# A mixture-of-experts layer with x and the weights laid out by the host, loaded by two queues, and the first products in another order

## The reference

```python
def _L0_cond_ref(hidden_states, gating_probs, shared_gate_prob, Wg, Wu, Wd, Sg, Su, Sd):
    E, B, S, D, F = (8, 2, 128, 128, 512)     # B is 16 here: x is (16, 128, 128)
    h = hidden_states
    g = jnp.einsum('bsd,edf->ebsf', h, Wg)
    u = jnp.einsum('bsd,edf->ebsf', h, Wu)
    expert_outs = jnp.einsum('ebsf,efd->ebsd', jax.nn.silu(g) * u, Wd)
    expert_output = jnp.einsum('be,ebsd->bsd', gating_probs, expert_outs)
    shared = jnp.einsum('bsf,fd->bsd', jax.nn.silu(h @ Sg) * (h @ Su), Sd)
    sg = shared_gate_prob[:, :, None]
    return (1.0 - sg) * expert_output + sg * shared

def _L1_cond_ref(x, fwd_steps, T):
    Tb = T[fwd_steps - 1]
    return jnp.einsum('bij,bjk->bik', Tb, x)

x = x + _L0_cond_ref(x, ...)
x = x + _L1_cond_ref(x, itok_B_1_98, L1_cond_T)
```

## Time and profile before

| what | value |
|---|---|
| median of 3 runs | 311.98 us (311.73 to 312.07) |
| the profiled execution, its own time | 312.09 us |
| its span in the trace | 310.1 us |
| PE busy | 305.5 us, 99% of the span |
| DVE, ACT, POOL busy | 217.5, 164.6, 102.2 us |
| moved by the DMA engines | 10.39 MB |

### The profile page before, as it was taken

One profiled execution on the slowest core, in us unless ns is written; L12 is line 12 of the kernel. 1 busy time (PEld: TensorE's weight loads), 2 busy tenths in 40 slices (PEclk: granted clock), 3 DMA queues, 4 the chain that ended last, 5 costly groups with the idle time before them and its releaser, 6 DMA issues.

```text
span 310.1 us, 4762 instructions
## 1 busy us (share of the span) xinstructions
PE 305.5 (99%) x1364; PEld 253.3 (82%) x1364; DVE 217.5 (70%) x355; ACT 164.6 (53%) x306; POOL 102.2 (33%) x116
## 2 busy tenths in 40 slices
PE   8999999999999999999999999999999999999996
PEld 7688888888888888888888888888888888888885
DVE  2786667766676666776667766677666766668885
ACT  5565555555555555555555555555555555555552
POOL 2565312441155115511552134411441155111310
PEclk9999999999999999999999999999999999999999
DMA  6930300030001100030003001100013000000112
GB/s 159 201 89 2 103 1 2 0 94 7 1 0 45 56 0 0 0 101 0 0 0 109 13 13 17 17 14 13 15 17 110 0 0 0 0 2 0 34 36 68
DMA packets 32727, 10.39 MB, mean 34 GB/s; under 512 B 16208, under 2 KB 32720, under 8 KB 32720
## 3 DMA queue, kind: packets, MB, share of 16 engines
q1 hardware_dynamic: 32720, 10.30, 13.5%
HBM read 9.25 MB, written 1.05 MB: 33 GB/s over the span
## 4 chain that ended last, share of the span: by engine, by line
PE 95%; SPq 1%; DMA 1%; POOL 0%; DVE 0%; ACT 0%; issue 0%
PE o_bank L470 11%; PE o_bank L473 11%; PE o_bank L471 11%; PE g_bank L446 10%; PE u_bank L446 10%; PE g_bank L445 10%; PE u_bank L445 10%; PE g_bank L444 10%; PE u_bank L444 10%; DMA w_raw<-in_L_cond_Wd 1%; PE o_bank L491 1%; SPq L158 1%; PE o_bank L483 0%; POOL w_lo L212 0%; DVE res L371 0%; PE u_bank L483 0%
## 5 line engine op out<-in xcount | busy, mean ns | idle before, releaser
L342 DVE TENSOR_TENSOR u_bank<-u_bank,silu_g 128x512 f32<-128x512 f32 x144 | 100.7, 699 | 84.2 <-PE u_bank L446 82.6
L278 ACT ACTIVATE silu_g<-g_bank 128x512 f32<-128x512 f32 x144 | 86.1, 598 | 132.8 <-PE g_bank L446 132.4
L348 DVE TENSOR_TENSOR h_lo<-u_bank,h_hi 128x512 fp32r<-128x512 f32 x144 | 97.9, 680 | 0.1
L260 POOL TENSOR_TENSOR acc<-acc,scaled 128x512 f32<-128x512 f32 x32 | 41.5, 1296 | 163.2 <-DVE scaled L356 163.0
L284 ACT ACTIVATE h_hi<-u_bank 128x512 fp32r<-128x512 f32 x144 | 85.4, 593 | 0.7 <-DVE u_bank L342 0.7
L470 PE MATMUL o_bank<-h_hi,w_hi 128*128 128x512 f32 x144 | 56.2, 390 | 0.8 <-POOL w_lo L212 0.8
L444 PE MATMUL u_bank<-x_hi,w_hi 128*128 128x512 f32 x144 | 56.1, 390 | 0.0
L473 PE MATMUL o_bank<-h_lo,w_hi 128*128 128x512 f32 x144 | 56.0, 389 | 0.0
L445 PE MATMUL u_bank<-x_lo,w_hi 128*128 128x512 f32 x144 | 56.0, 389 | 0.0
L471 PE MATMUL o_bank<-h_hi,w_lo 128*128 128x512 f32 x144 | 56.0, 389 | 0.0
L446 PE MATMUL u_bank<-x_hi,w_lo 128*128 128x512 f32 x144 | 56.0, 389 | 0.0
(11 more groups left out here) (49 smaller groups left out, 151.2 us busy)
## 6 DMA issues: line engine op xcount, KB each, us to landing
w_raw<-in_L_cond_Wd SPq DMA_DIRECT2D x8, 256.0 KB, 3.9
w_raw<-in_L_cond_Wg SPq DMA_DIRECT2D x7, 256.0 KB, 3.1
w_raw<-in_L_cond_Wu SPq DMA_DIRECT2D x7, 256.0 KB, 3.8
T_blk<-in_L_cond_T SPq DMA_DIRECT2D x64, 16.0 KB, 1.6
out_y<-res SPq DMA_DIRECT2D x3, 256.0 KB, 2.3
x_blk<-in_x SPq DMA_DIRECT2D x4, 128.0 KB, 3.6
x_nat<-in_x SPq DMA_DIRECT2D x1, 256.0 KB, 2.8
x_blk<-in_x SPq DMA_DIRECT2D x4, 64.0 KB, 2.7
```

The costliest lines, as they stand in the source:

```text
L260: nc.gpsimd.tensor_tensor(acc[:, t, :], acc[:, t, :], scaled[:, t % 2, :], ALU.add).then_inc(acc_done, 1)
L278: nc.scalar.activation(silu_g[:, k % 2, :], g_bank[k % 2][:, :], ACT.Silu).then_inc(g_read, 1)
L342: nc.vector.tensor_tensor(u_bank[k % HR][:, :], u_bank[k % HR][:, :], silu_g[:, k % 2, :], ALU.mult).then_inc(h_done, 1)
L348: nc.vector.tensor_tensor(h_lo[:, k % HR, :], u_bank[k % HR][:, :], h_hi[:, k % HR, :].bitcast(F32), ALU.subtract).then_inc(split_done, 1)
```

## The change

The host now hands over other layouts. `xT` is x with the features in front, so a tile is 128 rows of 2 KB and lands in `acc` itself. `W_all` holds for each expert, row and chunk the gate, up and down columns side by side, so an expert is one transfer. `TT` is T with each matrix turned, and it lands in `T_plus`, where POOL adds the identity in place. `side` holds gates and shares, repeated for all rows. The output is stored as rows, batches, features and turned on the host. The transposes of x and T on PE and DVE, and their buffers, are gone.

```diff
-            sp.dma_start(x_nat[:, :, :], x[0:BT, :, :].rearrange("b s d -> s b d")).then_inc(x_in[0], 16)
-            sp.dma_start(w_raw[:, 0, 0, 0, :], Wg[0, :, 0:P]).then_inc(wg0_in, 16)
-            sp.dma_start(w_raw[:, 0, 0, 1, :], Wu[0, :, 0:P]).then_inc(wu0_in, 16)
...
-            load_blocks(x_blk[:, BT:2 * BT, :], x[BT:2 * BT, :, :], [x_in[1]] * 4)
-            sp.dma_start(w_raw[:, 0, :, 2, :], Wd[0, :, :].rearrange("(c p) d -> p c d", p=P)).then_inc(wd0_in, 16)
...
+            load_x(0, 1, x_in[0])
+            sp.dma_start(w_raw[:, 0, 2:NC, 0:2, :], W_all[0, :, 2:NC, 0:2, :]).then_inc(wc0_in[2], 16)
+            sp.dma_start(w_raw[:, 0, :, 2, :], W_all[0, :, :, 2, :]).then_inc(wd0_in, 16)
+            load_x(1, 2, x_in[1])
+            sp.dma_start(side_b[:, :], side).then_inc(c_in, 16)
+            load_x(2, NT, x_in[2])
+            load_expert(1, slice(1, 2))
...
+            for c in range(2):
+                act.dma_start(w_raw[:, 0, c, 0:2, :], W_all[0, :, c, 0:2, :]).then_inc(wc0_in[c], 16)
             act.wait_ge(zero_done, 1)
             nc.scalar.activation(silu_0[:, :], zero[:, 0:1], ACT.Silu)
...
+            for c in range(2):
+                act.wait_ge(wc0_in[c], 16)
+                round_w0(c, slice(0, 2))
...
+            dve.wait_ge(x_in[0], 16)
+            nc.vector.tensor_copy(x_hi[:, 0, :], acc[:, 0, :]).then_inc(x_rounded, 1)
             dve.wait_ge(x_rounded, 1)
+            nc.vector.tensor_tensor(x_lo[:, 0, :], acc[:, 0, :], x_hi[:, 0, :].bitcast(F32), ALU.subtract).then_inc(split_done, 1)
+            dve.wait_ge(w0_rounded, 2)
+            nc.vector.tensor_tensor(w_lo[:, 0, 1, 0:2, :], w_raw[:, 0, 1, 0:2, :], w_hi[:, 0, 1, 0:2, :].bitcast(F32),
                                     ALU.subtract).then_inc(split_done, 1)
+            dve.wait_ge(wc0_in[2], 16)
+            nc.vector.tensor_copy(w_hi[:, 0, 2:NC, 0:2, :], w_raw[:, 0, 2:NC, 0:2, :]).then_inc(split_done, 1)
...
             pe.wait_ge(zero_done, 1)
             warm_up(6)
...
+            pe.wait_ge(x_rounded, 1)
+            for c in range(2):
+                pe.wait_ge(w0_rounded, c + 1)
+                high(g_bank[c][:, :], c, 0)
+                high(u_bank[c][:, :], c, 1)
             pe.wait_ge(split_done, 1)
             pe.wait_ge(w_ready, 1)
+            low(g_bank[0][:, :], 0, 0).then_inc(g_done, 1)
+            low(u_bank[0][:, :], 0, 1).then_inc(u_done, 1)
+            pe.wait_ge(split_done, 2)
+            low(g_bank[1][:, :], 1, 0).then_inc(g_done, 1)
+            low(u_bank[1][:, :], 1, 1).then_inc(u_done, 1)
```

More of the change, by code:

```diff
@@ L14, in moe_then_step_kernel @@
     nc: bass.Bass,
-    x: bass.AP,
-    route: bass.AP,
-    share: bass.AP,
+    xT: bass.AP,
+    side: bass.AP,
     step: bass.AP,
[L19 to L25, removed]
+    W_all: bass.AP,
+    TT: bass.AP,
     out: bass.AP,
 ):
-    B, S, D = x.shape
-    E, _, F = Wg.shape
-    K = T.shape[0]
+    S, B, D = out.shape
+    E = W_all.shape[0] - 1
+    NC = W_all.shape[2]
+    K = TT.shape[0]
     assert S == P and D == P
-    NC = F // P
     BT = 4
@@ L55, in moe_then_step_kernel @@
     EARLY = 3
-    Q = 32
     assert NC == 4 and NT == 4 and E % 2 == 0
@@ L96, in moe_then_step_kernel @@
         x_in = [sem(f"x_in{i}") for i in range(3)]
-        wg0_in = sem("wg0_in")
-        wu0_in = sem("wu0_in")
-        w0_in = sem("w0_in")
+        wc0_in = [sem(f"wc0_in{i}") for i in range(3)]
         wd0_in = sem("wd0_in")
@@ L102, in moe_then_step_kernel @@
         c_in = sem("c_in")
-        T_in = [sem(f"T_in{q}") for q in range(P // Q)]
+        T_in = sem("T_in")
         zero_done = sem("zero_done")
@@ L154, in _ @@
         def _(sp):
[L155 to L164, removed]
@@ L199, in _ @@
                 sp.wait_ge(res_done, last + 1)
-                sp.dma_start(out[b0:b1, :, :].rearrange("b s d -> s b d"), res[:, b0:b1, :]).then_inc(stored, 16)
+                sp.dma_start(out[:, b0:b1, :], res[:, b0:b1, :]).then_inc(stored, 16)
             sp.wait_ge(stored, 16 * (NT + 1))
@@ L292, in round_x @@
             def round_x(t):
-                act.wait_ge(x_turned, t)
+                act.wait_ge(x_in[min(t, 2)], 16)
                 nc.scalar.activation(x_hi[:, t, :], acc[:, t, :], ACT.Copy).then_inc(x_rounded, 1)
@@ L425, in _ @@
                 split_h(n - 1, n - 1)
-                if n in TURN_T:
-                    t = TURN_T.index(n)
-                    if t == 0:
-                        for q in range(P // Q):
-                            dve.wait_ge(T_in[q], 16 * B)
-                    tile = slice(t * BT, (t + 1) * BT)
-                    nc.vector.transpose(T_turn[:, tile, :].rearrange("p b s -> p (b s)"),
-                                        T_blk[:, tile, :].rearrange("p b s -> p (b s)")).then_inc(T_turned, 1)
             dve.wait_ge(o_done, E * NT + NT)
@@ L501, in _, with high, low @@
             warm_up(6)
-            pe.wait_ge(ident_done, 2)
-            pe.wait_ge(x_in[0], 16)
-            for j in range(BT):
-                last = nc.tensor.transpose(o_bank[0][:, j * S:(j + 1) * S], x_nat[:, j, :], ident[:, :])
-            last.then_inc(x0_turned, 1)
-            warm_up(2)
+            def high(bank, c, m):
+                nc.tensor.matmul(bank, w_hi[:, 0, c, m, :], x_hi[:, 0, :], start=True, stop=False)
+            def low(bank, c, m):
+                nc.tensor.matmul(bank, w_hi[:, 0, c, m, :], x_lo[:, 0, :], start=False, stop=False)
+                return nc.tensor.matmul(bank, w_lo[:, 0, c, m, :], x_hi[:, 0, :], start=False, stop=True)
             pe.wait_ge(x_rounded, 1)
-            nc.tensor.matmul(g_bank[0][:, :], w_hi[:, 0, 0, 0, :], x_hi[:, 0, :], start=True, stop=False)
+            for c in range(2):
+                pe.wait_ge(w0_rounded, c + 1)
+                high(g_bank[c][:, :], c, 0)
+                high(u_bank[c][:, :], c, 1)
             pe.wait_ge(split_done, 1)
-            nc.tensor.matmul(g_bank[0][:, :], w_lo[:, 0, 0, 0, :], x_hi[:, 0, :], start=False, stop=False)
-            pe.wait_ge(split_done, EARLY)
-            nc.tensor.matmul(g_bank[0][:, :], w_hi[:, 0, 0, 0, :], x_lo[:, 0, :], start=False, stop=True).then_inc(g_done, 1)
-            project_u(0, 0)
             pe.wait_ge(w_ready, 1)
-            product(g_bank[1][:, :], (0, 1, 0), x_hi[:, 0, :], x_lo[:, 0, :], True, True).then_inc(g_done, 1)
-            project_u(1, 1)
+            low(g_bank[0][:, :], 0, 0).then_inc(g_done, 1)
[3 more added lines that the diff above has]
+            low(u_bank[1][:, :], 1, 1).then_inc(u_done, 1)
             with pe.Fori(0, N_ROUTED // U, 2) as e:
```

110 lines of the change are left out of this document (45 added, 65 removed).

## The result

The changed kernel is slower, by a little: 312.86 us median (311.35 to 313.93, 20 runs) against 311.68 (311.21 to 312.73, 20 runs), a ratio of 1.0032 with a 95% interval of 1.002 to 1.0044. Its runs lie 2.6 us apart, those of before 1.5, and they fall into two groups: three of the twenty took 311.35 to 311.61 us, the other seventeen 312.32 or more. The execution that was profiled took 311.43 us and is the second shortest of the 20, so its trace does not show what the median is about. Both have to be explained: what this trace shows, and why most executions are not like it.

The account below looks back on a forecast made before the run. PE was taken to bound the kernel, busy 305.5 of 310.1 us. From 312.09 us, -1.25 for an earlier first down product and -0.1 for the tail gave 310.7, range 310.0 to 312.2.

Parts of the forecast that it names:

- where the clock rises: PE's first products: five at 0.42 us from 4.9, the sixth at 7.0, where TensorE's clock goes to its higher level.
- a rival at 0.27: PE's start: idling 0.9 us delays the clock's rise, each us costing 0.45; rise at 9.0 gives 311.4; chance 0.27.
- the start that I had assumed: PE's first product at 4.9 us: x at 4.1, its copy 0.68, and 0.1 for two handovers.
- When x is there: Load of x's tile 0: lands at 3.54 to 4.4 us, taken as 4.1, sharing the engines with ACT's queue.
- Its weights are earlier: First product's weights: chunk 0 is ready about when x lands, and its rounding fits before 4.9 us.
- The tail: Last stores: runs of 1 or 2 KB instead of 512 B save 0.1 us, bounds 0 and 0.2.
- The copy of x: DVE's copy of x to `x_hi` before the first product: 0.68 us, bounds 0.29 to 0.70.
- The base: Starting time of the sum: the profiled execution's 312.09 us, 0.11 above the runs' median of 311.98.
- this chain decides: First down product at 10.2 us: set by silu, ACT's rounding at 8.15 and POOL; PE, ready at 10.0, waits 0.2.

Follow-up runs that it names:

- e5_tile_rows: Changed kernel with x laid out by the host as contiguous 256 KB tiles and nine matmuls on zeros instead of six: 310.42 us, ratio 0.9957.
- e12_out_tiles: Changed kernel with contiguous tiles of x, nine matmuls on zeros, and each stored output tile as one contiguous block: 309.97 us, ratio 0.9941.
- e9_tile_out: Changed kernel with contiguous tiles of x, nine matmuls on zeros, and output stored in rows of 512 B: 310.26 us, ratio 0.9953.

## Why the prediction was wrong

I forecast 310.7 us, faster, and it is 312.86, slower. The range of 310.0 to 312.2 doesn't hold it. Two steps of the sum failed, the clock and the landing of x, and each alone is enough to undo the gain: with either one put right the kernel takes 311.6, as before the change.

**The step that failed first: "where the clock rises", at 7.1.** The sum took the time at which the clock rose in one execution of the kernel before and used it for the changed kernel. With PE idle for 0.9 us that assumption alone costs 1.2 us: 311.61 against 310.42, with the first product where I had it. With the real gap of 1.9 us it costs 1.26 (312.86 against 311.60). I had this as a rival at 0.27, priced at 0.45 us for each us of delay, and the price is about right: in the profile with the gap of 0.94 us the clock rose some 5.3 us later than in that with nine zeros (10.6 against 5.3), which by the price is 2.4 us less the wait that it covers, and the first down product came 2.0 us later (11.81 against 9.79). What was wrong is the weight. Nothing had been shown that a gap is harmless; I argued that it was short beside the work around it, and it was not. The early clock of my sum is what 3 of 20 executions had, and 2 of 12 at the start that I had assumed.

The rule of the Trainium skill that I had cited (TensorE: Matmul & The Clock Gate, Part 1) says that the point differs from run to run, since the monitor isn't reset with the kernel. The traces agree: two kernels whose PE starts alike, nine zeros and a first product at 4.96 and 4.92, have their clock up at about 5.3 (e5_tile_rows) and at about 7 (e12_out_tiles, whose products start at 6.35, 6.78, 7.14 and 7.37). One trace's 7.1 was no number to build on.

**The second step that failed: "When x is there", 3.54 to 4.4.** Measured 5.1, outside my bounds, which costs 1.2 us of the time (311.60 against 310.42). Of the 1.6 us by which x lands later than before, sharing with ACT's queue is some 0.4 us (first chunks on SP) and the pitch of 8 KB about 1.0 (contiguous tiles). My bounds came from the rate in a window of the kernel before, whose transfers read short rows at a small pitch, and the host's new layout was treated as free. This also made PE's gap twice as long.

**"Its weights are earlier".** Wrong for this kernel: chunk 0 landed at 5.34 and was what PE's first product waited for, and chunk 1 at 6.33 cost PE more, 0.59 us from the second product's start to the third's instead of 0.23.

**The tail, -0.1.** Wrong in sign. Stores with rows 8 KB apart cost 0.42 us more than rows of 512 B. The sum's argument, that fewer and longer rows can only help, left out where the rows lie.

**The copy of x, 0.68.** Measured 0.43. The row I went by reads PSUM; the page of the Trainium skill (VectorE: DVE Perf Modes, "The perf-mode tier table") gives 0.42 by my estimate, and the trace agrees.

**The base, 312.09.** I took the profiled execution to lie 0.11 us above the median. Against 20 runs it lies 0.41 above, so part of the forecast gain was never there.

**What was right.** In the changed kernel's trace ACT rounds the down weights directly behind silu of unit 0, not behind a transfer, and POOL follows. That this chain decides was right only in part: PE's own products end within 0.1 us of it, and with contiguous tiles the down weights, landed at 7.71 where I had put them at 6.0, decide in one trace. From the first down product on nothing else moved: it came 0.84 us earlier in the profile, the last copies of the result 0.81 us. The transposes of x and T on DVE and the single transfer per expert gave nothing, as said. In the profiled execution, where the clock had risen early, the whole change gives 0.66 us (312.09 to 311.43), and that is what a single trace would have told. With both layouts and the zeros put right (e9_tile_out) the kernel takes 310.26 us, 1.38 under the kernel before beside it, where the forecast had a gain of 1.39. That the two agree so well is partly luck: the copy was 0.25 us shorter than my term and the first down product came at 9.79 instead of 10.2, while the base was 0.4 too high.

So the sum that fits the median is: about 0.8 us gained at the first down product, 0.4 us lost in the stores, and 1.3 us, on the median, lost to the late clock, against 1.2 us measured. The three don't add up exactly (they give 0.9). What is left, 0.3 us, is about the 0.41 us by which the profiled execution of the kernel before lies above its median, so that the 0.8 is probably too much; no run shows this.

## What to carry to other kernels

When a change makes PE start its products earlier or its warm-up shorter, look at whether PE still has work without a pause up to the first product; fill up with matmuls on zeros, which cost nothing as long as they stand in a wait (311.60 instead of 312.86 here), and look at the spread of the runs, not at one trace. When the host lays out data for a kernel, make what one transfer moves one contiguous block: longer rows at a large pitch were slower than short rows in one block, in loads and in stores. A stretch that PE runs slowly may cost nothing as long as it sits in front of a longer wait, and it is to be priced anew when that wait goes.

## What the runs showed of the hardware

- With a pause of 0.94 us between PE's matmuls on zeros and its products the clock rose only at about 10.6 us in one execution, and the median of twelve was 1.2 us over that with three more zeros and no pause. The granted clock of the windows read 1.00 all the while; only the distance of starts showed it.
- With such a pause the executions of one kernel fall into two groups about 1 us apart (3 low and 17 high in the changed kernel, 4 and 8 with the first chunks on SP, 2 and 10 with contiguous tiles; all 11 high where SP held back). In the profiled ones of the low groups (311.43 and 310.79 us) the zeros ran at the lower clock up to 3.99 us and the first product after an idle stretch of 1.7 to 1.9 us ran at the higher: the clock can rise while PE is idle.
- The first 256 KB of x took 4.4 us to land with rows of 2 KB at a pitch of 8 KB, 3.4 us with the same rows in one block. A store of 128 KB took 2.4 us with rows 8 KB apart, 2.1 us in rows of 512 B in one block, 1.8 us in long rows in one block.
- POOL's low part of 128x256 took 1.05 us beside DVE's subtraction of two SBUF operands, and 0.74 us before. The other way round, in the kernel with short rows, DVE's copy took 0.76 us instead of 0.43 when POOL's operation had begun first.
